# A fused group norm and windowed ratio: a product moved ahead at the batch boundary, the last duo in other banks and in halves

## What is computed

```python
g = group_norm(x, G=32, eps=1e-5)        # mean and variance over h, w and the 6 channels of a group
s = box_sum(g, axis=2, w=5)              # sliding sums along w, zero padded
num = box_sum(s * s, axis=3, w=20)       # along the channels
d = box_sum(box_sum(g * g, axis=2, w=5), axis=3, w=20)
out = x + nan_to_num(num / (d * norm), nan=1.0)   # norm: how many columns a window of 5 covers
```

## Time and profile before

| | |
|---|---|
| median of 3 runs | 382.54 us (382.38 to 382.55) |
| the profiled execution: time, span | 381.17 us, 379.5 us |
| TensorE matmuls, weight loads: busy | 355.8 us (94%), 349.5 us (92%) |
| VectorE, ScalarE, GpSimd: busy | 298.4 us (79%), 273.1 us (72%), 249.5 us (66%) |
| mean granted TensorE clock | 0.998 of full speed |
| HBM read, written | 25.17 MB, 25.17 MB |

### The profile page before, as it was taken

One profiled execution on the slowest core, in us unless ns is written; L12 is line 12 of the kernel. 1 busy time (PEld: TensorE's weight loads), 2 busy tenths in 40 slices (PEclk: granted clock), 3 DMA queues, 4 the chain that ended last, 5 costly groups with the idle time before them and its releaser, 6 DMA issues.

```text
span 379.5 us, 7832 instructions
## 1 busy us (share of the span) xinstructions
PE 355.8 (94%) x2960; PEld 349.5 (92%) x2960; DVE 298.4 (79%) x609; ACT 273.1 (72%) x383; POOL 249.5 (66%) x168
## 2 busy tenths in 40 slices
PE   1999979999999999999869999999999999999982
PEld 1999969999999999999869999999999999999981
DVE  2999964766679999999957877777778877777774
ACT  1455559989999999987726777777777777777751
POOL 4000064887888888887158877788777787777631
PEclk9999999999999999999999999999999999999999
DMA  8999300588999973222202222211222222222214
GB/s 243 327 328 329 105 2 0 168 252 263 290 281 282 287 241 106 85 85 83 85 0 85 85 84 85 82 54 53 64 85 85 83 85 85 83 86 83 66 53 134
DMA packets 66486, 50.84 MB, mean 134 GB/s; under 512 B 912, under 2 KB 66448, under 8 KB 66448
## 3 DMA queue, kind: packets, MB, share of 16 engines
q1 hardware_dynamic: 66448, 50.34, 42.8%
HBM read 25.17 MB, written 25.17 MB: 133 GB/s over the span
## 4 chain that ended last, share of the span: by engine, by line
PE 71%; DVE 7%; ACT 5%; issue 2%; POOL 1%; DVEq 0%; POOLq 0%; ACTq 0%
PE N L529 21%; PE U L520 17%; PE D L529 14%; PE S L520 11%; PE S L529 4%; DVE late_triples L668 3%; PE D L572 3%; ACT xs L455 1%; DVE ratio L776 1%; DVE N L779 1%; ACT q L473 1%; ACT xc L422 1%; POOL xc L358 1%; ACT q L479 1%; DVE ratio L785 1%
## 5 line engine op out<-in xcount | busy, mean ns | idle before, releaser
L364 POOL TENSOR_TENSOR xs<-xs,ratio 128x768 f32<-128x768 f32 x63 | 114.6, 1820 | 63.4 <-DVE ratio L785 63.4
L358 POOL TENSOR_TENSOR xc<-xs,mean_c 128x768 f32<-128x768 f32 x64 | 116.9, 1829 | 44.8 <-DVE mean_c L677 44.8
L776 DVE SCALAR_TENSOR_TENSOR ratio<-D,q 128x768 f32<-128x768 f32 x51 | 48.6, 952 | 43.0 <-ACT q L479 43.0
L785 DVE SCALAR_TENSOR_TENSOR ratio<-ratio,N 128x768 f32<-128x768 f32 x64 | 61.1, 954 | 6.4
L779 DVE SCALAR_TENSOR_TENSOR N<-N,q 128x768 f32<-128x768 f32 x64 | 61.5, 960 | 4.9 <-PE N L529 3.1
L473 ACT ACTIVATE q<-D 128x768 f32<-128x768 f32 x51 | 41.4, 811 | 28.1 <-PE D L529 18.4
L479 ACT ACTIVATE q<-q 128x768 f32<-128x768 f32 x64 | 54.1, 846 | 2.0
L520 PE MATMUL S<-b,xc 128*128 128x128 f32 x432 | 54.0, 275 | 0.0
L529 PE MATMUL N<-b_r,xs 128*128 128x138 f32 (+2 forms) x384 | 52.4, 285 | 0.0
L529 PE MATMUL N<-b,xs 128*128 128x138 f32 (+2 forms) x384 | 51.7, 283 | 0.3 <-DVE ratio L785 0.3
L446 ACT ACTIVATE xs<-S 128x768 f32<-128x768 f32 x36 | 29.2, 812 | 31.5 <-PE S L520 31.5
(11 more groups left out here) (89 smaller groups left out, 452.6 us busy)
## 6 DMA issues: line engine op xcount, KB each, us to landing
out<-xs SPq DMA_DIRECT2D x31, 768.0 KB, 3.8
xs<-x SPq DMA_DIRECT2D x8, 1536.0 KB, 14.8
xs<-x SPq DMA_DIRECT2D x16, 768.0 KB, 5.3
out<-xs SPq DMA_DIRECT2D x2, 384.0 KB, 2.6
```

The source lines that it names most:

```text
L358: nc.gpsimd.tensor_tensor(pairs(xc[:, n % XC_RING, :]), pairs(x_flat(n)), mean, ALU.subtract)\
L364: nc.gpsimd.tensor_tensor(x_flat(n), x_flat(n), ratio[:, n % RATIO_RING, :], ALU.add)\
L776: nc.vector.scalar_tensor_tensor(t1, in_bank(d_bank(n)), -TINY, pairs(q[:, n % Q_RING, :]), ALU.add, ALU.mult).then_inc(t1_ready, 1)
L785: nc.vector.scalar_tensor_tensor(t1, t1, 2.0, in_bank(N), ALU.add, ALU.mult).then_inc(ratio_ready, 1)
```

## The change

At the boundary, TensorE's N(29) comes ahead of the mean's product, which gets its own semaphore and goes beside U (second bank) in place of N; it waits for the copy of U(31), and U(32) waits for ssq_c. `spread_late` runs right behind t1(29), ahead of t2(29). GpSimd finishes duo 28 and clears its sums before it waits for the mean. At the end, D(63) goes into S and N(63) into U; their waits are for the square of S(63) and the copy of U(63). VectorE forms ratio(63) in place in U and adds it to x one pair at a time, and SP stores each pair (two rows of x) behind its addition.

```diff
-        mean_ps = [D[:, 1, 6 * GROUPS:7 * GROUPS], beside[1][:, 0:GROUPS]]
+        mean_ps = [D[:, 1, 6 * GROUPS:7 * GROUPS], U[:, 1, PCOLS:PCOLS + GROUPS]]
...
-            return S if n < SWAPPED and n % 2 else D
+            return S if n < SWAPPED and n % 2 or n == LAST else D
+        def n_bank(n):
+            return U if n == LAST else N
...
-            last = TOTAL - 1
-            sp.wait_ge(out_ready, last)
-            sp.dma_start(dram_rows(out, last - 1), x_rows(last - 1)).then_inc(stored[1], 16)
-            sp.wait_ge(tail_ready, 1)
-            sp.dma_start(dram_rows(out, last), x_rows(last)).then_inc(stored[0], 16)
-            sp.wait_ge(stored[0], 16 * (BATCH * STEPS // 2 + 1))
+            sp.wait_ge(out_ready, LAST)
+            sp.dma_start(dram_rows(out, LAST - 1), x_rows(LAST - 1)).then_inc(stored[1], 16)
+            for i in range(DUO):
+                first = ROWS - DROWS + i * PAIR
+                sp.wait_ge(tail_ready, i + 1)
+                sp.dma_start(out[BATCH - 1, first:first + PAIR, :, :].rearrange("h w c -> w h c"),
+                             x_rows(LAST)[:, i * PAIR:(i + 1) * PAIR, :]).then_inc(stored[0], 16)
+            sp.wait_ge(stored[0], 16 * (BATCH * STEPS // 2 + DUO))
...
                 if m == DUOS:
+                    finish(n)
+                    clear_sums()
                     for j in range(len(LATE_SETS)):
                         wait_loaded1(pool, j)
                     pool.wait_ge(mean_ready, 2)
-                    clear_sums()
                 if m < TOTAL:
                     centre(m)
                 if summed(m):
                     normalise(m)
-                finish(n)
+                if m != DUOS:
+                    finish(n)
...
+                if n == MEAN_AT + BOX_AHEAD + 1:
+                    pe.wait_ge(ssq_ready, 2)
...
             def sum_d(n):
                 pe.wait_ge(us_ready, n + 1)
-                if d_prev(n) >= 0:
+                if n == LAST:
+                    pe.wait_ge(s2_ready, n + 1)
+                elif d_prev(n) >= 0:
                     pe.wait_ge(t1_ready, d_prev(n) + 1)
...
             def sum_n(n):
                 pe.wait_ge(s2_ready, n + 1)
-                if n:
+                if n == LAST:
+                    pe.wait_ge(us_ready, n + 1)
+                elif n:
                     pe.wait_ge(ratio_ready, n)
                 else:
                     pe.wait_ge(edges_ready, 2)
-                if n == MEAN_AT:
-                    average_late_means()
                 if n == VAR_AT:
                     average_squares(1)
-                box20(N, s2_of(n), batch(n)).then_inc(n_ready, 1)
+                box20(n_bank(n), s2_of(n), batch(n)).then_inc(n_ready, 1)
...
             def average_late_means():
+                pe.wait_ge(us_ready, MEAN_AT + BOX_AHEAD + 1)
                 pe.wait_ge(mean_sum_ready, 1)
...
                 sum_n(n)
+                if n == MEAN_AT:
+                    average_late_means().then_inc(late_mean_in_psum, 1)
...
             def spread_late():
+                dve.wait_ge(late_mean_in_psum, 1)
                 spread_mean(1)
...
                                                ALU.add, ALU.mult).then_inc(t1_ready, 1)
+                if behind_t1:
+                    behind_t1()
                 dve.wait_ge(n_ready, n + 1)
...
+            def finish_last():
+                q_of, t1, t2, rows = [pairs(a) for a in (q[:, LAST % Q_RING, :], ratio[:, LAST % RATIO_RING, :])] + [
+                    in_bank(n_bank(LAST)), pairs(x_flat(LAST))]
+                dve.wait_ge(q_ready, LAST + 1)
+                dve.wait_ge(out_ready, LAST - RATIO_RING + 1)
+                nc.vector.scalar_tensor_tensor(t1, in_bank(d_bank(LAST)), -TINY, q_of, ALU.add, ALU.mult)\
+                  .then_inc(t1_ready, 1)
+                dve.wait_ge(n_ready, LAST + 1)
+                nc.vector.scalar_tensor_tensor(t2, t2, TINY, q_of, ALU.add, ALU.mult).then_inc(t2_ready, 1)
+                dve.wait_ge(t1_ready, LAST + 1)
+                dve.wait_ge(t2_ready, LAST + 1)
+                for i in range(DUO):
+                    link(nc.vector.scalar_tensor_tensor(t2[:, i, :], t1[:, i, :], 2.0, t2[:, i, :], ALU.add, ALU.mult))
+                    nc.vector.tensor_tensor(rows[:, i, :], rows[:, i, :], t2[:, i, :], ALU.add).then_inc(tail_ready, 1)
...
-                quotient(n, before_ratio=spread_late if n == MEAN_AT else scale_late_bands if n == VAR_AT else
-                         spread_scale if n == VAR_AT + 1 else None)
+                quotient(n, behind_t1=spread_late if n == MEAN_AT else None,
+                         before_ratio=scale_late_bands if n == VAR_AT else spread_scale if n == VAR_AT + 1 else None)
...
-            n = TOTAL - 1
-            quotient(n)
-            dve.wait_ge(ratio_ready, n + 1)
-            nc.vector.tensor_tensor(x_flat(n), x_flat(n), ratio[:, n % RATIO_RING, :], ALU.add).then_inc(tail_ready, 1)
+            finish_last()
```

More of the change, by code:

```diff
@@ L32 @@
 TOTAL = BATCH * DUOS
+LAST = TOTAL - 1
 SPAN = [(max(128 * j - C_HI, 0), min(128 * (j + 1) + C_LO, PCOLS)) for j in range(CHUNKS)]
@@ L158, in window_ratio_kernel @@
         mean_in_psum = sem("mean_in_psum")
+        late_mean_in_psum = sem("late_mean_in_psum")
         offsets_in_psum = sem("offsets_in_psum")
@@ L571, in sum_d @@
                     pe.wait_ge(of_20_ready, nth_summed(n) + 1)
-                    mm = nc.tensor.matmul(D[:, 1, 0:PCOLS], b5d[:, :], of_20, start=True, stop=True)
+                    mm = nc.tensor.matmul(d_bank(n)[:, 1, 0:PCOLS], b5d[:, :], of_20, start=True, stop=True)
                 mm.then_inc(d_ready, 1)
@@ L766, in mend_edges, with quotient @@
                 ins.then_inc(edges_ready, 1)
-            def quotient(n, before_ratio=None):
+            def quotient(n, behind_t1=None, before_ratio=None):
                 if summed(n + 2):
```

## The result

The changed kernel takes 376.08 us (median of 4 runs, 375.89 to 377.26) against 382.55 us before (382.38 to 382.74): ratio 0.9837, 95% interval 0.9816 to 0.9858. The forecast was 377.4, 376.7 to 378.7. The direction was right and the size was not: 6.5 us went, not 5.1.

A forecast was written before the change was run, and what follows sets the result against it. TensorE was taken to bound the kernel, with slack only at the batch passage and the last duo. Gains of 2.19 + 1.0 and 1.58 - 0.25 + 0.6 made 5.1 us, so 377.4 us, range 376.7 to 378.7.

The forecast's parts named there:

- What bounds: Whole kernel: TensorE is full from 207 to 365 us, so a gain or loss ahead of it reaches the end whole.
- N(29), copies, clearing: Passage between batches: mean ready 2.19 us earlier, clearing ahead of the wait gives 1.0; U(32) at 194.7, together 3.2 us.
- Later work is in the same order as before, so the 3.2 us lasts: From passage to tail: the 3.2 us stays unchanged, with TensorE full.
- Banks: Last duo: D(63) into S starts t1(63) 1.58 us earlier, bounds 1.45 to 1.65; N(63) into U gives nothing.
- Halves and store: Last duo: ratio and addition in halves lose 0.25 us; the last store in two gains 0.6 us.
- the overlap: VectorE's half operations: unlinked successive ones overlap by 0.08 us; with no overlap the loss would be 0.33 us.
- The median of the runs, 382.54, is 1.37 above that execution, and I keep this distance: Last step of the sum: 376.05 us for the profiled execution becomes a median of 377.4 us.
- rival W: In e3's forecast: the 1.4 us are lost elsewhere, at a place the change doesn't touch; no chance given.
- the store's time: Rival at the end: landing time is fixed at 2.6 us; gain 4.5 us, time 378.0, chance 0.14.
- VectorE wasn't the new wait: Rival at the passage: VectorE makes U(32) or N(30) late by 0.5 to 1.5 us; time 378.4, chance 0.12.
- the mean was what U(32) waited for: Rival at the passage: U(32) waits for something else, only the tail's 1.9 us comes; time 380.6, chance 0.03.
- Slower: Rival at the passage: ratio(29), behind the variance chain, comes after 201.4 us and loses everything; 383.5 us, chance 0.01.

The follow-up runs named there:

- e4: The kernel before with GpSimd's order alone changed: duo 28 finished and sums cleared ahead of the wait for the mean; median 380.80 us, ratio 0.9961.
- f0: The changed kernel run again, unchanged, for more of its executions; median 376.57 us, ratio 0.9853 against before.
- f2: The kernel before with an unread product filling only TensorE's first pause at the passage (188.6 to 190.6 us); median 382.49 us, ratio 1.0027.
- l1: The changed kernel with an unread window product of raw duo 26 added in TensorE's early pause; median 375.83 us, ratio 0.9812 against before.
- e3: The kernel before, unchanged, to see its executions one by one; 12 executions from 381.19 to 384.35 us, median 382.10, the profiled one 384.35.
- first group: Follow-up kernels run on one chip beside before: whether and where executions differ, and the change's two halves apart; before's fastest there 381.06 us.
- f3: The kernel before with unread products filling only TensorE's second pause at the passage (195.3 to 197.9 us); median 382.03 us, ratio 0.9982.
- k1: The changed kernel with the real product of raw duo 26 moved into TensorE's early pause; median 377.41 us, ratio 0.9873 against before.
- k2: The changed kernel with raw duo 26's real product moved into the early pause and duo 32 centred, squared and multiplied in halves; median 377.08 us.
- f1: The kernel before with unread products in both of TensorE's pauses at the passage; median 381.07 us, ratio 0.9968.
- l3: The kernel before with unread products in three pauses, the early one and the two at the passage; median 380.93 us, ratio 0.9956.
- e2: The kernel before with the last duo's part of the change alone (banks, halves, two stores); median 380.35 us, ratio 0.9947.

## Why the prediction was right and where it failed

**What bounds.** Right: the 3.25 us won at U(32) came through to the end.

**N(29), copies, clearing.** Right. The copies began at 191.08 (191.3 forecast), centring at 191.92 (192.0), U(32) at 194.66 (194.7), the squares at 196.26 (196.3). Clearing alone (e4) gave 1.04 for 1.01, of which 0.17 can come from N(31), next.

**"Later work is in the same order as before, so the 3.2 us lasts".** Short by 0.17. Before, N(31) took 1.62 us by the chain, with a wait for ratio(30) in it; after, it takes 1.45, and D(62) starts 3.41 us earlier (364.87 to 361.46). Why is in the last section; the rows of before and of e4:

```profile
205.97 1.62 PE N L529 x12
```

```profile
205.69 1.45 PE N L531 x12
```

**Banks.** Right: t1(63) is 4.93 us earlier, less 3.41 is 1.52 (1.58, bounds 1.45 to 1.65). It waits for ScalarE's q; ratio(62) is through at 367.54, 0.08 before.

**Halves and store.** Right: the last addition ends at 371.77, 4.66 earlier, so the halves cost 0.27 (0.25); landing 2.0 us for 2.6. Together 3.41 + 1.52 - 0.27 + 0.6 = 5.26, and the span went from 379.5 to 374.2.

On the overlap, the prediction took from the Trainium skill, "VectorE: DVE Perf Modes", section "The DRAIN you can't avoid", that there is none. The same section adds that a next operation which isn't held starts earlier. That fits the trace: the second half's ratio, which waits for nothing, starts at 370.62 in the timeline, where the first addition ends at 370.71. On the store, by the Trainium skill's fit for GpSimd's path ("DMA: Bandwidth & Descriptors", section "Anatomy of one DMA — SWDGE (gpsimd) path") 192 KB would land in an estimated 2.45 us. SP's store took 2.0, so the fit doesn't carry over, and the measurement decides.

**The step that failed: "The median of the runs, 382.54, is 1.37 above that execution, and I keep this distance".** The distance isn't a constant around the kernel. It is what falls of TensorE's clock cost in most executions of before, behind three pauses: this change shortens two of them, and the early one stays. The term was taken over whole from before to after. The profiled execution had no fall ahead of TensorE's last product. In the changed kernel's first four, three have a time without one (375.89, 375.98, 376.17), and the median is 0.19 above its profile; in f0's six it is 0.69 above the fastest. The term for the changed kernel was thus 0.2 to 0.7 us and not 1.37, which gives 376.2 to 376.7 by the median.

A part of the 6.5 us may be the luck of the draw. No clock of before's four executions (382.38 to 382.74) is on record, so which pause lengthened them is open; f2's six at 382.21 to 382.51 show that such times come with the first pause filled, too. In f0's group, with 28 executions of before and six of the changed kernel, the medians are 5.9 us apart. The early pause, the place where f2's trace and l1 find the rest, is one that the change doesn't touch: rival W of e3 is right in part.

The prediction read the clock at 1.00 through the pause of 193.60 to 197.90 and concluded that pauses don't matter to it. That window couldn't tell: in e3's trace it has 1.00 as well, and the clock falls at 199.3, 1.3 us behind it. One execution couldn't show it either, while the runs, all three 1.2 us and more above the profiled one, said that it wasn't typical. Nor is 0.8 us what a measurement of this kernel tells from nothing: executions of before lie from 381.06 to 386.08 in the first group alone.

None of the rivals happened: the store's time fell with its size, VectorE wasn't the new wait, the mean was what U(32) waited for, and ratio(29) came at 195.51. The clock was named in the one called "Slower" and dismissed.

## What to carry to other kernels

Look at how the profiled execution stands to the runs before using it. If they differ by more than the runs differ among themselves, something varies from execution to execution, and the pauses of TensorE are a place to look; a change that shortens them can gain more than the chain shows. Look at the clock behind a pause and not in it. Filling a pause with added products tests this in one run and can itself be worth keeping (l1: 375.83 for 376.57 in f0), while moving real work into one only moved the pause here.

## What was unexpected of the hardware

**Short pauses can halve the clock.** Behind pauses of 2.66 us (e3), of 1.94 us (f3, e4), of 2.17 us at 47 us (f2) and of 1.71 us (k1) the granted clock fell to 0.50, and these executions are 0.7 us (e4) to 3.2 us (e3) longer than the fastest of their kernel, f2's with its two falls 4.1. Behind the same pauses of 2.66 and 1.94 us in the first profile of before, of 1.71 us in k2's and of 2.27 and 2.39 us at 47 us in e3's and f0's it stayed at 1.00. With 0.49 and 0.97 us left at the passage and 1.16 at the early place (in the profiled one), none of l1's six executions shows a fall in its time. The Trainium skill, "TensorE: Matmul & The Clock Gate", section "HAM oscillation — how this bites in real kernels", says that PE idling while it waits can let the clock drop, so that the next piece of work starts cold. The traces agree, with pauses shorter than the waits of 3 to 5 us in that section's example. Why one execution is spared and the next isn't, with the same pause, no run here shows.

**A VectorE instruction held beside GpSimd.** The three scalings of the bands (L718 before, L737 after), with GpSimd's centring next to them, in before's timeline and in the one after:

```profile
202.25 1.82 POOL L358 TENSOR_TENSOR xc<-xs,mean_c 128x768 f32<-128x768 f32 x1
...
203.16 1.41 DVE L718 TENSOR_SCALAR b<-b,inv_var 128x138 f32<-128x138 f32 x3
```

```profile
197.36 1.83 POOL L367 TENSOR_TENSOR xc<-xs,mean_c 128x768 f32<-128x768 f32 x1
...
199.91 0.70 DVE L737 TENSOR_SCALAR b<-b,inv_var 128x138 f32<-128x138 f32 x3
```

They took 1.41 us where GpSimd was centring at their start, and 0.70 where it had gone idle at 199.19. f1's and l3's traces have 1.43 and 1.41 beside a centring; e3's, with GpSimd idle, has 0.70. In before's rows by shape one of the three takes 1.00 us and the others 0.28; the first starts at 203.16, so it ends at 204.16, 0.09 behind the centring. The nearest to a test is e4, which changes nothing but GpSimd's order: GpSimd is idle there, the scalings take 0.70 us and N(31) 1.45. In before, e2, f1, f3 and l3 they take 1.41 to 1.43 and N(31) 1.62 to 1.64. That is the 0.17 us that my sum lacked. The Trainium skill, "SBUF — State Buffer", section "Who interferes with whom", says that an instruction of this kind, when it runs in a mode with two ports, and GpSimd lock each other out of a shared pair of ports. These rows agree; whether the three ran in such a mode no row shows.
